# Routed expert blocks in pairs, halves split before the transposes, and both shared passes ahead of the first routed pass, in a layered f32 kernel

## The reference

```python
x = x + 0.5 * _L0_ffn_ref(_layernorm(x, axis=-1), ...)
x = x + _L0_attn_ref(_layernorm(x, axis=-1), ...)
x = x + 0.5 * _L0_ffn_ref(_layernorm(x, axis=-1), ...)
x = x + 0.5 * _L1_ffn_ref(_layernorm(x, axis=-1), ...)
x = x + _L1_attn_ref(_layernorm(x, axis=-1), ...)
x = x + 0.5 * _L1_ffn_ref(_layernorm(x, axis=-1), ...)
```

```python
combine = (jax.nn.one_hot(topk_idx, E, dtype=x.dtype) * topk_w[..., None]).sum(1)
shared = _silu_mul(x @ shared_gate_up.T, SI) @ shared_down.T
shared = shared * jax.nn.sigmoid(x @ shared_gate_vec.T)
def step(acc, ew):
    w_gu, w_d, cw = ew
    h = _silu_mul(x @ w_gu.T, I)
    return (acc + h @ w_d.T * cw[:, None], None)
```

## Time and profile before

| | us |
|---|---|
| runs | 996.26, 999.32, 1001.56 |
| median | 999.32 |
| profiled execution | 1001.14 |
| its span in the profile | 999.3 |
| PE busy | 876.1 (88%) |
| DVE busy | 746.2 (75%) |
| ACT busy | 474.8 (48%) |
| POOL busy | 424.5 (42%) |
| granted PE clock, mean share | 0.955 |

### The profile page before, as it was taken

How to read it: one execution, slowest core, us unless ns; L and a number is a source line. 1 busy time by engine, 2 the same in 40 slices (tenths; PEclk the granted TensorE clock), 3 DMA queues, 4 the chain that set the end, 5 groups by cost and what they waited for, 6 DMA issues and landing times.

```text
span 999.3 us, 19391 instructions
## 1 busy us (share of the span) xinstructions
PE 876.1 (88%) x6148; PEld 537.4 (54%) x6148; DVE 746.2 (75%) x1636; ACT 474.8 (48%) x981; POOL 424.5 (42%) x402
## 2 busy tenths in 40 slices
PE   4375899999838899979789989899999999999997
PEld 2143665656524566646565546454566545666564
DVE  6777465798888978854886787878878789775554
ACT  4646443467723667534654773235433453332332
POOL 2783037501385522148711987531342324423232
PEclk9778999999959989989999999999999999999999
DMA  9769545433121224665973542121110211112121
GB/s 314 271 202 271 138 137 133 125 83 97 49 75 58 80 50 95 210 172 123 222 180 106 167 148 69 45 76 43 43 53 33 77 43 53 54 40 91 65 73 64
DMA packets 128207, 110.60 MB, mean 111 GB/s; under 512 B 76648, under 2 KB 102888, under 8 KB 128112
## 3 DMA queue, kind: packets, MB, share of 16 engines
q1 hardware_dynamic: 121968, 92.58, 32.1%
q0 software_dynamic: 6144, 16.79, 6.0%
HBM read 58.98 MB, written 34.08 MB: 93 GB/s over the span
## 4 chain that ended last, share of the span: by engine, by line
PE 49%; DVE 8%; issue 4%; POOL 3%; DMA 2%; ACT 2%; POOLq 0%; DVEq 0%; SPq 0%; ACTq 0%
PE ps L1037 21%; PE ps L1081 10%; PE ps L1011 5%; PE ps L1059 3%; PE ps L1224 2%; DVE hid L1295 1%; PE ps L1046 1%; DVE x L1455 1%; POOL wlo L763 1%; DMA xs_sb<-xs_dram 1%; PE ps L1258 1%; POOL back L752 1%; PE ps L1244 1%; POOL hlo L713 1%; PE ps L1234 1%
## 5 line engine op out<-in xcount | busy, mean ns | idle before, releaser
L713 POOL TENSOR_TENSOR hlo<-hid,hhi 128x512 f16<-128x512 f32 x120 | 142.0, 1185 | 269.3 <-ACT hhi L818 268.9
L1295 DVE SCALAR_TENSOR_TENSOR hid<-gtanh,ps 128x176 f32<-128x176 f32 (+1 forms) x244 | 123.4, 506 | 135.8 <-ACT gtanh L801 119.3
L801 ACT ACTIVATE gtanh<-ps 128x176 f32<-128x176 f32 (+1 forms) x244 | 110.1, 451 | 205.2 <-PE ps L1037 160.0
L1037 PE MATMUL ps<-xhi,whi 128*128 128x512 f16 x480 | 185.7, 387 | 20.7 <-DVE hid L1295 19.8
L1037 PE MATMUL ps<-xlo,whi 128*128 128x512 f16 x480 | 185.6, 387 | 0.0
L1037 PE MATMUL ps<-xhi,wlo 128*128 128x512 f16 x480 | 185.4, 386 | 0.0
L1011 PE MATMUL ps<-whi,xs_sb 128*128 x496 | 118.3, 325 | 26.2 <-DVE hid L1311 10.7
L1081 PE MATMUL ps<-whi,hhi 128*128 128x256 f16 x480 | 132.6, 276 | 5.5 <-POOL hlo L713 5.5
L1311 DVE SCALAR_TENSOR_TENSOR hid<-hid,ps 128x176 f32<-128x176 f32 (+1 forms) x244 | 122.8, 503 | 16.9 <-PE ps L1037 11.6
L1081 PE MATMUL ps<-wlo,hhi 128*128 128x256 f16 x480 | 132.4, 276 | 0.0
L1081 PE MATMUL ps<-whi,hlo 128*128 128x256 f16 x480 | 132.2, 275 | 0.0
(11 more groups left out here) (216 smaller groups left out, 1745.5 us busy)
## 6 DMA issues: line engine op xcount, KB each, us to landing
ys_dram<-y_sb SPq DMA_DIRECT2D x124, 128.0 KB
xs_sb<-c_dram SPq DMA_DIRECT2D x64, 192.0 KB, 2.7
scr<-w_in SPq DMA_DIRECT2D x28, 384.0 KB, 4.9
scr<-we_in SPq DMA_DIRECT2D x32, 304.0 KB, 5.2
xs_sb<-c_dram SPq DMA_DIRECT2D x64, 128.0 KB, 2.9
xs_dram<-y_sb SPq DMA_DIRECT2D x2, 3968.0 KB, 16.7
xs_sb<-c_dram SPq DMA_DIRECT2D x64, 64.0 KB, 2.7
scr<-ws_in SPq DMA_DIRECT2D x8, 384.0 KB, 5.2
```

Of the source, the lines that this page charges most:

```text
L713: pool.tensor_tensor(hlo[:, k, :], hid[:, k % 2, :], hhi[:, k, :], ALU.subtract).then_inc(lo_done, 1)
L801: act.activation(gtanh[:, n % 2, 0:w], ps[:, bank, 0:w], ACT.Tanh, scale=0.5 / W_SCALE)\
L1037: mm = pe.matmul(ps[:, bank, :], w[:, off:off + P], a[:, kc, t0:t0 + HN], start=(i == 0), stop=(i == 3 * KC - 1))
L1295: dve.scalar_tensor_tensor(out=hid[:, k, 0:w], in0=gtanh[:, k, 0:w], scalar=1.0, in1=gate, op0=ALU.add, op1=ALU.mult).then_inc(act_done, 1)
```

## The change

- `PASSES` now starts shared half 0, shared half 1, routed half 0, routed half 1.
- A unit of a routed pass is a pair of blocks: 16 units for 31 blocks (`NRT`), the last with one block. `xs_loads(c)` is its number of blocks. Rings become 3 pairs for x, 2 pairs for y, 6 for the gathered rows; the register ring is 4 pairs of two (`REGS`).
- Gate and up of a pair are two pieces: 12 matmuls of 176 columns into the bank of gate, 12 into that of up. There is one bank of each, shared with the dense units: gate waits for `act_done` of the unit before, up for `h_ready`.
- `hid` is split before the transposes: ACT makes hi (128 x 2 x 176) from SBUF, POOL makes lo (in place of DVE). PE transposes both as f16: per block one 128 x 128 for each and two 64-row pieces for the last 64 columns (112 + 64 = 176), placed side by side so that hi and lo of the remainder share one block. `hT_copy` on ACT brings 768 columns to SBUF. `down` has five matmuls of 256 columns per block in place of six, with the down weights laid out for it.
- The zeroing matmuls are gone: the first matmul into each bank carries the start flag.
- All five order strings are written anew. The positions of the scatter (`pos`, one table per half) are as they were.

```diff
-XRING, YRING, GRING = 6, 3, 8
+XRING, YRING, GRING = 3, 2, 6
...
-REGS = 6
+REGS = 4
...
-PASSES = [(SH, 0, 0), (RT, 0, 0), (SH, 0, 1), (RT, 0, 1), (SH, 2, 0), (RT, 2, 0), (SH, 2, 1), (RT, 2, 1),
+PASSES = [(SH, 0, 0), (SH, 0, 1), (RT, 0, 0), (RT, 0, 1), (SH, 2, 0), (RT, 2, 0), (SH, 2, 1), (RT, 2, 1),
...
             put("PE", "t", "turn", u)
-            put("DVE", "l", "lo", u)
+            put("ACT", "u", "hT_copy", u)
...
-                        sp_.wait_ge(gate_ready, n - XRING + 1)
+                        sp_.wait_ge(up_ready, n - XRING + 1)
...
+                        pool.tensor_tensor(hp[:, j, 0:w, 1, 0:I0], hid[:, n % 2, 0:w * I0].rearrange("p (b i) -> p b i", i=I0),
+                                           hp[:, j, 0:w, 0, 0:I0], ALU.subtract).then_inc(lo_done, 1)
...
-                        act.wait_ge(turned, BLOCK[r] + c + 1)
-                        act.wait_ge(down_done, n - 3)
-                        act.activation(hhi[0:IH, k, 0:2 * P], ps[0:IH, T_BANK, 0:2 * P], ACT.Copy).then_inc(hi_done, 1)
+                        act.wait_ge(h_ready, n + 1)
+                        if m >= 2:
+                            act.wait_ge(turned, m - 1)
+                        act.activation(hp[:, m % 2, 0:w, 0, 0:I0], hid[:, n % 2, 0:w * I0].rearrange("p (b i) -> p b i", i=I0),
+                                       ACT.Copy).then_inc(hi_done, 1)
...
+                    act.wait_ge(turned, BLOCK[r] + c + 1)
+                    if n >= 4:
+                        act.wait_ge(down_done, n - 3)
+                    act.activation(hh[:, n % 4, 0:w], ps[:, T_BANK, :].bitcast(F16)[:, 0:w], ACT.Copy).then_inc(hT_done, 1)
...
-                    pe.reg_load(at_expert[k], eoff[0:1, h, c:c + 1])
...
-                    pe.wait_ge(h_ready, n if c == 0 and PASSES[r - 1][0] != RT else n - 1)
...
-                            mm = pe.matmul(ps[:, m % 2, 0:2 * I0], xs_sb[:, slot, part + kc, :],
-                                           w[:, ds(offset[k] + (EXP0 + kc * 2 * I0), 2 * I0)],
+                        pe.wait_ge(down_done, n - REGS + 1)
+                        for j in range(xs_loads(c)):
+                            pe.reg_load(at_expert[k + j], eoff[0:1, h, 2 * c + j:2 * c + j + 1])
...
+                        pe.wait_ge(act_done, n)
...
+                        bank, part, done = G_BANK, 0, gate_ready
+                    else:
+                        pe.wait_ge(h_ready, n)
+                        bank, part, done = U_BANK, I0, up_ready
...
+                                mm = pe.matmul(ps[:, bank, j * I0:(j + 1) * I0], xs_sb[:, slot + j, a + kc, :],
+                                               w[:, ds(offset[k + j] + (EXP0 + kc * 2 * I0 + part), I0)],
...
-                    for j in range(2):
-                        mm = pe.transpose(ps[0:IH, T_BANK, P * j:P * j + P], hid[:, n % 2, IH * j:IH * (j + 1)], ident)
+                        for out, part in ((hT[:, at:at + P], hp[:, m % 2, b, 0, 0:P]),
+                                          (hT[:, at + P:at + 2 * P], hp[:, m % 2, b, 1, 0:P]),
+                                          (hT[0:IB, at + 2 * P:at + 3 * P], hp[:, m % 2, b, 0, IA:I0]),
+                                          (hT[IB:P, at + 2 * P:at + 3 * P], hp[:, m % 2, b, 1, IA:I0])):
+                            mm = pe.transpose(out, part, ident16[:, :])
...
-                        for b in range(2):
-                            pe.matmul(ps[:, ACC + b, :], zero16[:, :], xhi[:, 0, HN * PASSES[r][2]:HN * PASSES[r][2] + HN],
-                                      start=True, stop=False, skip_group_check=True)
...
-                        for a, w in ((hhi, whi), (hhi, wlo), (hlo, whi)):
+                        for m, (a, w) in enumerate(((hhi, whi), (hhi, wlo), (hlo, whi))):
-                                           start=False, stop=(c == NUM[r] - 1), skip_group_check=True)
+                                           start=(c == 0 and i % 2 == 0 and m == 0), stop=(c == NUM[r] - 1),
+                                           skip_group_check=True)
```

More of the change, by code:

```diff
@@ L38 @@
 SLOT_ROWS = NBLK * P
+NRT = -(-NBLK // 2)
 NW0 = NSH + 2 * E0 + 2
@@ L89, in make_threads @@
             put("SP", "y", "store_y", u)
-        else:
-            put("PE", "g", "up", u)
-            put("POOL", "l", "lo", u)
+        put("POOL", "l", "lo", u)
+        put("PE", "g", "up", u)
         put("ACT", "m", "hi", u)
@@ L1250, in piece @@
                         pe.wait_ge(gtanh_done, n + CC)
-                        for b in range(2):
-                            pe.matmul(ps[:, S0 + b, :], zero16[:, :], xhi[:, 0, 0:HN], start=True, stop=False,
-                                      skip_group_check=True)
                     pe.wait_ge(clo_done, n + 1)
```

183 lines of the change are left out of this document (98 added, 85 removed), and 106 rows, old and new, of the table ORDER.

## The result

The changed kernel took 1010.82 us (median of four; 1009.72 to 1017.36) against 999.86 for the kernel before, a ratio of 1.0128 with a 95% interval of 1.0076 to 1.018. The forecast was 963 with a range of 938 to 992. Its profiled execution took 1011.4 us with a span of 1009.6.

The account below looks back on a forecast made before the run. PE (88% busy) was taken to bound the kernel, with DVE pacing half 0's attention. Milestone gains of 16 at half 0's norm, 30, 44, then 37 at the dense gate gave span 964, median 963 us, range 938 to 992.

Parts of the forecast that it names:

- One routed block, PE: PE work of two routed blocks: 3.54 us before, 3.37 after; pair pace 4.2 to 4.5, so pairs alone gain 0.
- Register loads: Ahead of each routed gate: two offset loads in a row leave PE idle 0.7 to 0.9 us per pair.
- Start: Start to half 0's norm: shared half 1 fills idle PE time; first routed pass ends at 146, norm at 173.
- The stretch behind the first routed pass: Last down of that pass to half 0's norm: POOL's gathers set it, 27 us; norm at 173, gain 16.
- from 90: First routed pass after the last weight remainder: pairs' products, turns, gaps, router and start-up, last down at 146, 14 earlier.
- Attention: Both attention stretches: DVE's savings of 18.8 and 17, less 4 each, give 95 and 110 us.
- To the dense gate and dense: After attention: left-over blocks make 122 us to the first dense gate; dense passes 463.6, from 462.
- Shared port: DVE operations with two SBUF inputs and POOL's lock each other out; moving lo to POOL gives back part of the saving.
- (1): Rival: POOL's subtractions stop softmax on DVE under attention, 975, or the start gains nothing, 977; contention or start, chance 0.15.
- (3): Rival: with one gate bank, gate waits for DVE's act; pair pace 5.25, 48 us more, 1011; chance 0.08.
- (4): Rival: 176-column matmuls take 12 ns more than assumed, 18 us in all, 981; chance 0.03.
- (5): Rival: PE waits on softmax chains take what DVE frees; within 0.5% of 999; chance 0.06.

Follow-up runs that it names:

- e1: Changed kernel with every down matmul of a routed pair over all 128 rows; ratio 0.9988 to the kernel before, 998.0 us.
- e7: Kernel before with the second half of each routed block's down over 64 rows in place of 88; ratio 1.0128.
- e2: e1 plus three full 128 x 128 transposes per routed block, hi and lo interleaved (also written e2_turn3); ratio 0.9927, 990.5 us.
- e10: e2 measured again on kind 2, beside the changed kernel at 0.9971; ratio 0.9748.
- e3: Changed kernel with a pair's register loads put ahead of the up product of the pair before; ratio 1.0084.
- e4: e2 and e3 together, on the changed kernel; ratio 0.9955.
- e14_sp_all: e11_start with the first load of routed rows on SP behind 30 weight transfers; ratio 0.9889, 987.3 us.
- e6: Changed kernel with POOL's lower halves of routed pairs cut to 8 of 176 columns; ratio 1.0047 on kind 2, changed kernel 0.9971.
- e12: e11_start with POOL's lower halves of routed pairs cut to 8 of 176 columns; ratio 0.9788, e11_start beside it 0.971.
- e16_batch: e14_sp_all with the register loads of two pairs made at every second gate; ratio 0.9891.
- kind 1: Comparisons in which the kernel before took 997 to 998 us; ratios are compared only within a kind.
- e11_start: e2 with five of POOL's weight remainders put between the scatter groups at the start; ratio 0.971 on kind 2.
- kind 2: Comparisons in which the kernel before took 1031 to 1032 us; what makes the kind isn't known.

## Why the prediction was wrong, point by point

**One routed block, PE: the step that failed first.** "Turn 8 x 0.057 = 0.46, down 10 x 0.109 = 1.09". Each price was right for a matmul among its like. What was missing is the mix of shapes: 64 rows beside 112 or 128 cost 0.10 each way. Down measured 1.52 and turn 0.79. Gate and up took 2.13 to 2.22 together, where the sum had 1.82: the steps within a group of three matmuls are 0.08, but single ones between two groups are up to 0.23. Address operations stand there in the program; that they are the cause is a guess, and no run touched it, though 0.31 for 62 pairs is 19 us of PE, beside 27 for the down's 0.43 and 20 for the turn's 0.33. A pair took 5.02 in place of 4.2 to 4.5. For the down, e1 and e7 show the cause; with the turn's three transposes (e2, e10) it comes to about 20 us, 2.0 to 2.2%. With both edits the changed kernel is 0.7% faster than the one before.

**Register loads.** Forecast 0.7 to 0.9 of idle PE a pair; measured 0.46 to 0.70 (once 1.29), and 0.92 once the turn is short. The size was about right, and so was taking off what the turn covers; the wait for an earlier down was not what it hung on (e3, e4).

**Start: 173 forecast, 200.1 measured, the largest miss.** The stretch behind the first routed pass was right: 27 forecast, 27.9 measured. What failed is the sum before it, "from 90", with four pairs through gate and up by then and 56 us of PE and gaps left. The changed kernel and then the kernel before, up to 90 us and from there to the last down of the first routed pass (columns as in the earlier trace rows):

```profile
0.00:90.00 90.00, 62.51 (x441) 36.99 (x441) 69.15 (x141) 50.72 (x88) 54.50 (x61) 0.94 0.71 226
90.00:172.30 82.30, 70.76 (x633) 45.15 (x630) 33.39 (x71) 41.10 (x74) 37.43 (x37) 0.94 0.65 182
...
0.00:90.00 90.00, 49.16 (x278) 27.04 (x278) 62.45 (x131) 49.93 (x91) 50.86 (x58) 0.85 0.84 275
90.00:160.30 70.30, 60.72 (x446) 40.07 (x446) 41.74 (x129) 32.14 (x92) 20.42 (x20) 0.93 0.53 145
```

The first failed step is that 23.4 us of shared work go into idle PE time and the eight blocks become four pairs. In 90 us PE is busy only 13.3 more than before; the first routed gate comes at 82.3 (before 68.3), and by 90 only 45 of the pass's 372 gate and up matmuls are made, not two pairs, where the kernel before had eight blocks. The second is the price of a pair: the rest took 82, not 56, and PE was busy for 70.8 of it. "I let the last weight remainder end at 90" was wrong too, as POOL's ended at 105.9, but it isn't what held the pass: PE waited for POOL's remainders 2.3 us in all, and its idle time after 90 (11.5) is about what the sum had for gaps (10.8).

Why PE got less done by 90 is in part argued. I had left out the companions of the moved work: six more units are 6 x 1.37 on DVE, 6 x 1.2 on POOL and 6 x 1.2 on ScalarE, on the three engines that also make the weight halves. The 7.6 us that PE waits behind the lock fit this, but with the lock gone (e14_sp_all) the norm turn came only 2.9 earlier than in e2_turn3, and no run took the second shared pass back behind the first routed one. The cheaper down and turn brought 3.6 (200.1 to 196.5): between 90 us and the end of the pass PE is busy 11.7 less in e2_turn3, but idle 7.0 more. These are single profiles, and some 20 us of the miss stay open.

**Attention: 95 and 110 forecast, 105 and 119.6 measured.** DVE's routed work fell as summed, by 18.9 us (27.8 to 8.9) in the first. But its other work grew by 10, not 4, and the rule that DVE's share sets the stretch was too coarse. Two parts of the first attention stretch, changed kernel:

```profile
230.00:245.00 15.00, 14.43 (x160) 9.92 (x159) 13.28 (x32) 12.19 (x23) 3.91 (x5) 1.00 0.34 98
...
263.50:307.80 44.30, 23.79 (x237) 13.07 (x238) 35.31 (x85) 16.11 (x32) 28.38 (x31) 0.50 0.20 57
```

and the kernel before at the end of the same stretch:

```profile
274.90:302.10 27.20, 10.13 (x107) 5.80 (x108) 22.28 (x50) 5.90 (x12) 22.51 (x24) 0.50 0.27 76
```

Until 260 PE is full with routed pairs, so that DVE's saving can't show. From there softmax, gather and norm are left over and PE has little beside them. From 263.5 its granted clock stands at 0.50, the 1.2 GHz level, for 44 us, of which PE is busy 24 (before: for 27, busy 10). With the cheaper pair (e2_turn3) the stretch takes 99.4. The second takes 119.8 there, as long as without it, so the price of a pair is not what held that one. That the order strings decide both, more than any engine's sum, is a guess: no run changed them here.

**To the dense gate and dense: 122 and 463.6 forecast, 119.4 and 465.5 measured.** Right within 3 us, the first by luck: the pair was priced too low, and with the cheaper pair of e2_turn3 this stretch takes 113.4. (The forecast's own sum gives 963.6 for span and median alike, not 963; nothing hangs on it.)

**Shared port.** The lock was weighed with the right sign and the wrong place. By the Trainium skill (SBUF — State Buffer, "SBUF: two separate sides") whichever comes first has the port for a whole instruction. The measured 10.46 us lasts longer than any of POOL's instructions (1.2 to 1.4), and so did the 8.09 of the kernel before. In the changed kernel DVE got in only when POOL's run without a pause ended at 73.7. Under attention, where I priced it, e6 shows nothing and e12 leaves it open.

**Rivals.** (1) named "a start that stays" for 977; it was worse than that, the start lost 11. (3), one gate bank, has the right side and a wrong mechanism, and that its 1011 is the measured time is luck: PE's waits for act in routed stretches are 2.5 us from 95 to 200, and the pace of 5.0 came from the matmuls. (4), a floor for narrow matmuls, falls as a floor, at 0.08 within a group of three; but gate and up cost PE 19 us more than the sum, about its 18, by the longer steps between groups. (5) no. The zeroing matmuls were put at 4.3 us and were worth 0 to 3.

**What beats both kernels.** e14_sp_all (and e16_batch): 987 us against 997 on kind 1, e11_start 0.971 on kind 2; pairs stay, with full-width transposes and down.
